# Heads of three feed-forward blocks run tile by tile in the tail of the attention ahead of them

## What is computed

```
x = x + xattn0(layernorm(x))   # 32 heads, q and k RMS-normalised, added mask, output matrix
x = x + ffn0(layernorm(x))     # softmax routing of 8; (x * in_scale) @ sign(W).T * out_scale + bias
x = x + xattn1(layernorm(x))   # one narrow head
x = x + ffn1(layernorm(x))     # base plus a Fourier-coded low-rank update
x = x + xattn2(layernorm(x))   # 32 heads, mask and position bias
x = x + ffn2(layernorm(x))     # base plus 8 gated rank-16 adapters (softmax minus a threshold)
x = x + xattn3(layernorm(x))   # 32 query heads on 4 key heads
x = x + ffn3(layernorm(x))     # base plus 8 rank-16 adapters, the best two by a router
```

## Time and profile before

| | |
|---|---|
| median of 3 runs | 2523.36 us (2516.17 to 2525.8) |
| the profiled execution | 2523.6 us, its span 2521.8 us |
| mean granted TensorE clock | 0.953 |
| busy share: PE, PEld, DVE, ACT, POOL | 91%, 51%, 52%, 46%, 20% |
| chain that ended last, by engine | PE 62%, DVE 13%, ACT 11%, issue 11%, POOL 2%, DMA 1% |

### The profile page before, as it was taken

How to read it: one execution, slowest core, us unless ns; L and a number is a source line. 1 busy time by engine, 2 the same in 40 slices (tenths; PEclk the granted TensorE clock), 3 DMA queues, 4 the chain that set the end, 5 groups by cost and what they waited for, 6 DMA issues and landing times.

```text
span 2521.8 us, 40314 instructions
## 1 busy us (share of the span) xinstructions
PE 2285.4 (91%) x14182; PEld 1284.5 (51%) x14182; DVE 1315.1 (52%) x2618; ACT 1148.8 (46%) x2990; POOL 516.2 (20%) x889
## 2 busy tenths in 40 slices
PE   4899999999786788999999999998869899999979
PEld 2556555556432333555555555554634455555545
DVE  5566666666521144656556555655342455555551
ACT  4666665665211123555445555433222565555530
POOL 2333233232200011221212222111200121212130
PEclk9999999999778998999999999999879999999988
DMA  3111011010002121111111111100210110010000
GB/s 113 43 43 43 23 43 43 24 39 1 22 0 100 49 78 38 62 47 61 46 61 47 63 61 45 45 12 11 78 67 1 36 49 35 34 36 33 1 30 34
DMA packets 27622, 106.94 MB, mean 42 GB/s; under 512 B 4353, under 2 KB 12929, under 8 KB 17426
## 3 DMA queue, kind: packets, MB, share of 16 engines
q1 hardware_dynamic: 26962, 104.10, 11.7%
q10 hardware_dynamic: 448, 0.03, 0.0%
HBM read 102.03 MB, written 2.10 MB: 41 GB/s over the span
## 4 chain that ended last, share of the span: by engine, by line
PE 62%; DVE 13%; ACT 11%; issue 11%; POOL 2%; DMA 1%; ACTq 0%; DVEq 0%; POOLq 0%; SPq 0%
PE bank L84 16%; PE bank L86 15%; PE bank L85 15%; PE bank L1263 2%; ACT m_E L423 2%; PE bank L1592 2%; DVE m_x L867 2%; PE bank L614 2%; DVE m_Sm L821 2%; PE bank L1172 1%; ACT m_E L419 1%; PE bank L1377 1%; ACT m_arena L401 1%; DVE m_A L861 1%; ACT m_arena L296 1%
## 5 line engine op out<-in xcount | busy, mean ns | idle before, releaser
L767 DVE TENSOR_TENSOR m_arena<-bank,m_arena 128x512 f16<-128x512 f32 x320 | 221.1, 691 | 513.5 <-ACT m_arena L401 513.1
L84 PE MATMUL bank<-m_input_parts,m_arena 128*128 128x512 f16 x1088 | 418.5, 385 | 6.6 <-DVE m_arena L767 2.3
L85 PE MATMUL bank<-m_input_parts,m_arena 128*128 128x512 f16 x1088 | 418.2, 384 | 0.0
L86 PE MATMUL bank<-m_input_parts,m_arena 128*128 128x512 f16 x1088 | 418.1, 384 | 0.0
L423 ACT ACTIVATE m_E<-m_Sm,m_nmax 128x64 f32<-128x64 f32 (+1 forms) x512 | 185.4, 363 | 395.8 <-DVE m_nmax L838 219.9
L879 POOL TENSOR_TENSOR m_E<-m_E,m_rinv 128x512 f32<-128x512 f32 (+1 forms) x192 | 177.6, 925 | 871.3 <-DVE m_rinv L852 871.3
L401 ACT ACTIVATE m_arena<-bank 128x512 f16<-128x512 f32 x320 | 189.7, 593 | 237.9 <-PE bank L86 237.4
L84 PE MATMUL bank<-m_wo_t,m_A 128*128 128x512 f16 x768 | 293.3, 382 | 3.1 <-DVE m_x L867 3.1
L85 PE MATMUL bank<-m_wo_t,m_A 128*128 128x512 f16 x768 | 292.5, 381 | 0.0
L86 PE MATMUL bank<-m_wo_t,m_A 128*128 128x512 f16 x768 | 292.4, 381 | 0.0
L419 ACT ACTIVATE m_E<-bank,m_nmax,m_qk 128x128 f32<-128x128 f32 x256 | 113.7, 454 | 178.1 <-DVE m_nmax L809 178.1
(11 more groups left out here) (267 smaller groups left out, 4454.1 us busy)
## 6 DMA issues: line engine op xcount, KB each, us to landing
m_raw<-a_q SPq DMA_DIRECT2D x24, 1024.0 KB, 4.8
m_raw<-a_o SPq DMA_DIRECT2D x24, 1024.0 KB, 4.9
m_raw<-a_k SPq DMA_DIRECT2D x9, 1024.0 KB, 4.9
m_raw<-a_v SPq DMA_DIRECT2D x9, 1024.0 KB, 5.4
m_bias_in<-bias SPq DMA_DIRECT2D x64, 128.0 KB, 2.0
m_arena<-f_w SPq DMA_DIRECT2D x4, 1024.0 KB, 5.1
m_arena<-ctx_t SPq DMA_DIRECT2D x2, 2048.0 KB, 7.6
m_x<-x SPq DMA_DIRECT2D x2, 1024.0 KB, 7.0
```

The lines of the kernel that those rows point to most:

```text
L84: pe.matmul(out, lhs[0], rhs[0], start=first, stop=False)
L85: pe.matmul(out, lhs[0], rhs[1], start=False, stop=False)
L86: return pe.matmul(out, lhs[1], rhs[0], start=False, stop=last)
L767: ins = dve.tensor_tensor(self.dest(name, part, 1), self.shaped(name, bank[m % 2][:, :]), self.dest(name, part, 0), ALU.subtract)
```

## The change

`BinaryFFN` and `AdapterFFN` now derive from a new `TailFFN`, whose work on each tile stands in the events of period 8 of the attention ahead. `f_stat` is a tile's statistics and power, `f_norm` its normalising, transposes and copy, `f_logit` its narrow product, its copy and the bias addition. The gate's and A's products become one of 137 or 136 columns. The weights are loaded in the tail. `BinaryFFN` keeps x transposed, applies the input scale in that layout (eight-row products with 128 columns) and so has no transposes in its body; its output scale and main product get two banks each. `AdapterFFN` puts the base product in five banks, two of them filled in slot 7 of the tail, three more before the gates are needed. In `scales` the weight scale comes second in the chain, with a semaphore `w_fac` for the rest. The order in the list (the lines are those of `events`):

```diff
+            if t == 8 and slot == 0:
+                out.append(("f_stat", 0))
             if ok(b):
                 out.append(("scores", b))
+            if t == 8 and slot == 7:
+                out.append(("f_main", 0))
+            if t == 8:
+                out.append(("f_norm", slot))
+            if t == 8 and slot == 7:
+                out += [("f_main", 1), ("f_logit", 7)]
             if made is not None:
                 out.append(("w_sum", made, misc))
...
             if ok(b - 2):
                 out.append(("mix", b - 2))
+            if t == 8 and 1 <= slot < 7:
+                out.append(("f_logit", slot - 1))
+            if t == 8 and slot in (5, 6):
+                out.append(("f_gate" if slot == 5 else "f_route", 0))
             if ok(b - 3):
                 out.append(("out", b - 3))
+            if t == 8 and slot < 7:
+                out.append(("f_stat", slot + 1))
+            if t == 8 and slot == 6:
+                out.append(("f_logit", 6))
```

The shares of the engines in a tile:

```diff
+    def load_tail(self, sp):
+        s, a = self.s, self.att
+        sp.wait_ge(*a.s["proj_lo"].by(16 * a.NT))
+        sp.wait_ge(*a.s["misc_read"].by(a.misc_total))
+        for dst, src in self.small_loads():
+            sp.dma_start(dst, src).then_inc(s["w_in"].sem, 16)
+        for dst, src in self.wide_loads():
+            sp.dma_start(dst, src).then_inc(s["w"].sem, 16)
...
+    def tail_pool(self, pool, step, t):
+        k, s = self.k, self.s
+        if step == "f_stat":
+            pool.wait_ge(*s["stat"].by(t + 1))
+            pool.tensor_tensor(k.rstd[:, t:t + 1], k.var[:, t:t + 1], k.c_mhalf, ALU.pow).then_inc(s["rstd"].sem, 1)
+        elif step == "f_logit":
...
+            pool.tensor_tensor(k.x[:, t, :], k.x[:, t, :], self.bias[:, :], ALU.add).then_inc(s["xb"].sem, 1)
...
+    def tail_act(self, act, step, t):
+        k, s, bank = self.k, self.s, self.k.bank
+        if step == "f_norm":
+            act.wait_ge(*s["xt"].by(t + 1))
+            act.activation(self.xtf[:, :, t * P:(t + 1) * P], bank[t % 2][:, :].rearrange("p (c n) -> p c n", c=KC),
+                           ACT.Copy).then_inc(s["xt_s"].sem, 1)
+        elif step == "f_logit":
+            act.wait_ge(*s["lg"].by(t + 1))
+            act.activation(self.lg[:, t, :], bank[7][:, 0:self.G], ACT.Copy).then_inc(s["lg_s"].sem, 1)
...
+    def tail_dve(self, dve, step, t):
+        k, s, ch = self.k, self.s, self.ch
+        if step == "f_stat":
+            dve.wait_ge(*self.att.s["xadd"].by(UNITS - TILES + 1 + t))
+            dve.bn_stats(k.bn[:, t, :], k.x[:, t, :]).then_inc(ch.sem, 1)
...
+        elif step == "f_norm":
+            dve.wait_ge(*s["rstd"].by(t + 1))
+            dve.wait_ge(*s["xt"].by(t - 1))
+            dve.tensor_scalar(self.xn[:, t % 2, :], k.x[:, t, :], k.mv[:, t, 0:1], k.rstd[:, t:t + 1],
+                              ALU.subtract, ALU.mult).then_inc(s["xn"].sem, 1)
...
+    def tail_pe(self, pe, step, t):
+        k, s, bank = self.k, self.s, self.k.bank
+        if step == "f_norm":
...
+            pe.wait_ge(*s["xn"].by(t + 1))
+            pe.wait_ge(*s["xt_s"].by(t - 1))
+            for c in range(KC):
+                ins = pe.transpose(bank[t % 2][:, c * P:(c + 1) * P], self.xn[:, t % 2, c * P:(c + 1) * P], k.ident[:, :])
+            ins.then_inc(s["xt"].sem, 1)
+        elif step == "f_logit":
...
+            pe.wait_ge(*s["xt_s"].by(t + 1))
+            pe.wait_ge(*s["lg_s"].by(t))
+            for c in range(KC):
+                ins = pe.matmul(bank[7][:, 0:self.G], self.xtf[:, c, t * P:(t + 1) * P], self.narrow[:, c, :],
+                                start=c == 0, stop=c == KC - 1)
+            ins.then_inc(s["lg"].sem, 1)
```

TensorE's share of `BinaryFFN`'s body (its signs stand behind `f_norm` 1 to 4 on VectorE, the routing of tiles 0 to 3 in slots 5 and 6), and the order of `AdapterFFN` on TensorE:

```diff
+        for i in range(TILES + 1):
+            if i == 3:
+                self.turn_route(pe, 1)
             if i < TILES:
...
+                for c in range(KC):
+                    ins = pe.matmul(bank[4 + i % 2][:, c * P:(c + 1) * P], self.ics[:, c * P:(c + 1) * P], self.rt[:, tok],
+                                    start=True, stop=True)
+                ins.then_inc(s["insc"].sem, 1)
+                pe.wait_ge(*s["out_s"].by(i - 1))
...
+                pe.matmul(self.out_bank(i), self.rt[:, tok], self.ocs, start=True, stop=True).then_inc(s["outsc"].sem, 1)
+            if i >= 1:
                 j = i - 1
                 pe.wait_ge(*s["y"].by(j + 1))
+                pe.wait_ge(*s["x"].by(j - 1))
...
+    def main_bank(self, t):
+        return self.k.bank[2 + t % 5][:, :]
...
+        for t in range(2, 5):
+            self.base(pe, t)
+        pe.wait_ge(*s["xt_s"].by(TILES))
+        turn(0)
+        turn(1)
         for t in range(TILES):
             pe.wait_ge(*s["ht_s"].by(t + 1))
+            pe.matmul(self.main_bank(t), self.ht[:, t % 2, :], self.bm[:, :], start=False, stop=True).then_inc(s["main"].sem, 1)
             if self.follower and t % 2 == 0 and t // 2 < self.follower.NP:
                 self.follower.sum_ahead(pe, t // 2)
+            if t + 2 < TILES:
+                turn(t + 2)
+            if t + 5 < TILES:
+                self.base(pe, t + 5)
```

The scale chain:

```diff
         tt(sc, tot, k.c_mhalf, ALU.pow, t)
+        tt(sc, sc, k.c_cw, ALU.mult, t, s["w_scale"])
         tt(inv, tot, k.c_half, ALU.pow, t)
-        tt(inv, inv, k.c_icw, ALU.mult, t)
-        last = lambda: tt(sc, sc, k.c_cw, ALU.mult, t, s["w_scale"])
...
     def low(self, dve, kind, j, par, count):
         dve.wait_ge(*self.s["w_hi"].by(count))
+        dve.wait_ge(*self.s["w_fac"].by(count))
```

More of the change, by code:

```diff
@@ L285, in emit @@
                          at(t, self.NK, self.NP + n - 1))
+                if isinstance(t, int) and t == 8 and slot == 1:
+                    self.next.load_tail(sp)
         self.periods(sp, emit)
@@ L519, in emit @@
             for e in events:
-                if e[0] == "w_sum":
+                if e[0][:2] == "f_":
+                    self.next.tail_pe(pe, e[0], e[1])
+                elif e[0] == "w_sum":
                     _, n, misc = e
@@ L744, in emit @@
             for e in events:
-                if e[0] == "w_sum":
+                if e[0][:2] == "f_":
+                    self.next.tail_dve(dve, e[0], e[1])
+                elif e[0] == "w_sum":
                     _, n, misc = e
@@ L912, in scales @@
             tt(k.tmp, k.tmp, k.joint[:, 1:2], ALU.mult, t)
[L913 to L921, removed]
+            tt(k.qk[:, kp], k.tmp, k.c_scale, ALU.mult, t, fac)
+        else:
+            tt(inv, inv, k.c_icw, ALU.mult, t, fac)
     def pool_ahead(self, pool):
@@ L961, in emit @@
             for e in events:
-                if e[0] == "w_sum":
+                if e[0][:2] == "f_":
+                    self.next.tail_pool(pool, e[0], e[1])
+                elif e[0] == "w_sum":
                     _, n, misc = e
@@ L1380, in pe, with __init__, small_loads, wide_loads @@
                 self.follower.sum_ahead(pe, t // 2)
[L1383 to L1403 removed]
+class AdapterFFN(TailFFN):
+    def __init__(self, k, layer, att, dram):
+        n = P + (9 if layer == 2 else 8)
+        regions = [[k.arena, 12288, 13312], [k.arena, 16384, 24576]] if layer == 2 else \
+            [[k.arena, 12288, 16384], [k.joint_parts[:, 2 * KC * TOK:].bitcast(FP32), 0, 4096]]
+        super().__init__(k, f"f{layer}", ["iota", "hw", "ht", "ht_s", "out"], att, dram, n, regions)
+        self.layer = layer
+        self.w = self.take([KC, D])
+        self.bm = self.take([D])
+        self.hw, self.ht = self.take([TILES, P]), self.take([2, P])
+        self.z9, self.e9, self.z, self.e, self.g2, self.m8, self.oh = (self.take([72]) for _ in range(7))
+        self.idx, self.idf = self.take([64]), self.take([64])
+        self.nm, self.sm, self.thr, self.p1, self.p2 = (self.take([8]) for _ in range(5))
+        self.bthr, self.iota = self.take([1]), self.take([8])
+    def small_loads(self):
+        d = self.dram
+        out = [(self.narrow[:, :, :], d["narrow"]), (self.bias[:, :], d["bias"].partition_broadcast(P)),
+               (self.bm[:, :], d["bm"])]
+        if self.layer == 2:
+            out.append((self.bthr[:, :], d["bthr"].partition_broadcast(P)))
+        return out
+    def wide_loads(self):
+        return [(self.w[:, :, :], self.dram["w"])]
@@ L1562, in dve, with base @@
                     self.follower.low_ahead(dve, t // 2)
+    def main_bank(self, t):
+        return self.k.bank[2 + t % 5][:, :]
+    def base(self, pe, t):
+        s, a = self.s, self.att.s
+        if t == 0:
+            pe.wait_ge(*s["w"].by(16))
+            pe.wait_ge(*a["exped"].by(UNITS))
+        if t == 2:
+            pe.wait_ge(*a["turned_lo"].by(UNITS))
+            pe.wait_ge(*a["mixed_lo"].by(UNITS))
+            pe.wait_ge(*a["xadd"].by(UNITS))
+        pe.wait_ge(*s["xt_s"].by(t + 1))
+        pe.wait_ge(*s["x"].by(t - 4))
+        for c in range(KC):
+            pe.matmul(self.main_bank(t), self.xtf[:, c, t * P:(t + 1) * P], self.w[:, c, :], start=c == 0, stop=False)
@@ L1586, in turn @@
```

(13 more changed lines are left out.)

374 lines of the change are left out of this document (194 added, 180 removed).

## The result

| | before | after |
|---|---|---|
| median | 2524.07 us (20 runs, 2515.43 to 2526.95) | 2529.72 us (20 runs, 2523.03 to 2533.69) |
| span of the profiled execution | 2521.8 us | 2530.6 us |
| mean granted TensorE clock | 0.953 | 0.947 |

The ratio is 1.0025, with a 95% interval of 1.0018 to 1.0032: slower by a quarter of a per cent. The forecast was 2516, slightly faster.

What follows compares the result with a forecast made beforehand. Serial heads at a low clock make the blocks long; interleaved tails become one VectorE-TensorE loop. Tails +88.4, clock +42, blocks -134.5, weight scale -3 sum to -7.1 us: forecast 2516 us, own range 2500 to 2540, wider range 2472 to 2555.

Steps and rivals of the forecast that it cites:

- `BinaryFFN`'s block: Feed-forward block behind the first tail: 51.4 us instead of 110.2, saving 58.8, with 3 for starting at the lower clock level.
- the adapter blocks: AdapterFFN blocks: middle one 45.0 us instead of 78.3, last one 39.7 instead of 82.1.
- What bounds, and the loop: Attention tails: side-by-side work of VectorE and TensorE becomes one loop, slots with scores 8.7, 10.9 and 8.7 us.
- Rival C: Tails: the loop doesn't close, slots grow by statistics and hand-overs only, 1.6 us each; 2420 us, chance 0.07.
- The last three slots: Slots 4 to 6 of a tail: no scores, but exposed power and normalising beside POOL's bias addition; 8.5 us each.
- The clock, 2.0 us a slot: Tails: TensorE's idling lowers its clock, costing 2.0 us in each of 21 slots, 42 us.
- Rival A: Tails: the clock level holds and tails grow by their work alone; 2474 us, chance 0.17.
- Rival B: Tails: the lower clock lasts through each burst, 4.9 us in place of 2.0 in 21 slots; 2577 us, chance 0.15.
- Hidden pieces: Tails: ScalarE's copies, POOL's power and bias addition, signs and loads mostly covered; loads cost 0, at worst 5 us once.
- The blocks: Three feed-forward blocks behind the tails: savings of 58.8, 33.3 and 42.4 us, 134.5 in sum.
- The five banks: AdapterFFN blocks: five banks pay by letting the base products run ahead of the gates.
- The scales, -3: Earlier weight scale: most of ScalarE's 28.0 us wait lies beside TensorE work; -3 us, ends -8 and 0.

Runs made afterwards that it cites:

- run 6: Kernel after with ten 128 x 512 float16 matmuls on TensorE ahead of each tile's transposes (tiles 0 to 6): 2496.3 us, ratio 0.9895.
- run 3: Kernel after with TensorE's transposes of a tile and ScalarE's copy of them moved to the end of the slot, behind out: 2425.6 us, ratio 0.9615.
- run 9: Kernel after with AdapterFFN's base product in two banks instead of five, only slot 7's bases ahead of the gates: 2548.2 us, ratio 1.009.
- runs 1 and 2: New scale chain alone on the kernel before: 2515.2 us, ratio 0.9969; kernel after with the old scale chain: 2542.9 us, ratio 1.008.
- runs 6 and 8: Kernel after with ten matmuls ahead of each tile's transposes: 128 x 512 float16, 2496.3 us; float32 of 128 x 128 by 8 columns, 2534.9 us.
- run 7: Kernel after with fifteen 128 x 128 float32 transposes of the identity ahead of each tile's transposes: 2499.5 us, ratio 0.9903.
- run 2: Kernel after with the old scale chain (weight scale last, no w_fac): 2542.9 us, ratio 1.008.

## Why the prediction was wrong

The mechanisms held, and what failed are sizes in the sum, most of them by a little and to the same side. `BinaryFFN`'s block was put at 51.4 us and took 58.8; the adapter blocks took 4.2 more than forecast; the clock was put at 2.0 us a slot and cost about 2.3; the last three slots of a tail were put at 8.5 us and take 9.0 at the upper clock; and the second tail's first slot was 3.1 us longer. Only the term outside tails and blocks erred the other way.

**What bounds, and the loop.** Right. The slot closes into one loop through both engines, as the timelines of the first section show, and its three lengths are within 0.25 us of the forecast (run 6). Rival C is refuted for this order of the queue, for the reason given against it; its 2420 is nearly what run 3 (2425.6) reached once that order was changed.

**The last three slots, forecast 8.5 each.** With the wide matmuls the nine of them take 88.3 us in place of 76.5. Four (12.16, 11.05, 9.98 and 9.97) still had a clock of 0.72 to 0.85; the five at 1.00 are 8.6 to 9.5, on average 9.0. So some 5 us of the 11.8 are the loop and the other 7 are clock. For the loop a row of the kernel after has the reason. VectorE's normalising takes 1.48 us while GpSimd adds the bias, 0.54 elsewhere, so 0.94 more, where I had taken 0.3 as half of a difference read in an eight-tile batch. GpSimd's timeline and VectorE's, in the fifth slot of the first tail:

```profile
674.85 1.26 POOL L1141 TENSOR_TENSOR m_x<-m_x,m_arena 128x512 f32<-128x512 f32 x1
```

```profile
674.91 1.48 DVE L1165 TENSOR_SCALAR m_arena<-m_x,m_mv,m_rstd 128x512 f32<-128x512 f32 x1 [0.67 <-POOL m_rstd L1136]
```

The second attention's first slot was 3.1 us longer as well (13.24 against 10.1), because tile 0's statistics come 3.1 us after its addition, behind the last work of period 7. Finally, the second tail of before was cut 3.1 us short. That overstated its growth and cancelled this.

**The clock, 2.0 us a slot.** A little low: 42 us forecast, 37 to 49 measured and 48 by the estimate of run 6, which is 2.3 a slot. It was no single value: the same slot of the third tail takes 8.57 or 10.24 us, and slots of the first take 10.0, 11.9 or 13.1 against 8.60. Rival A (the level holds) is refuted. Rival B (the whole burst at 1.2 GHz) is true of single slots, as the one shown, 4.5 us longer than at the upper level, near its 4.9. Its break-even was 2.3 us a slot, which is about what the clock cost. So B's sign came out, with single slots and not every slot at its price.

**Hidden pieces.** ScalarE's copies put no wait on TensorE in the slot shown, and the loads cost nothing that shows: in the second tail the slot with the loads, at 160 GB/s, takes 13.99 us and the next one, with none, 13.82. GpSimd's pieces did cost what the forecast had put on the path, and the bias addition beside the normalising more than that.

**The blocks: -134.5 forecast, -123.0 measured.** This is the largest miss, and 7.4 us of its 11.5 are `BinaryFFN`: 58.8 us in place of 51.4. TensorE's timeline in that block:

```profile
711.72 1.12 PE L1176 MATMUL bank<-m_ident,m_arena 128*128 128x128 f32 x4 [3.33 <-DVE m_arena L1165]
713.52 1.88 PE L1185 MATMUL bank<-m_arena,m_input_parts 128*128 128x8 f32 x8 [0.69 <-ACT m_input_parts L1147]
715.33 2.07 PE L1329 MATMUL bank<-m_arena 8*128 8x128 f32 x8
...
722.45 5.93 PE L1342 MATMUL bank<-m_arena 128*128 128x512 f32 x8
...
747.42 3.70 PE L1342 MATMUL bank<-m_arena 128*128 128x512 f32 x8
751.05 1.15 PE L1329 MATMUL bank<-m_arena 8*128 8x128 f32 x8
752.04 1.02 PE L1336 MATMUL bank<-m_arena 8*128 8x512 f32 x2
```

A tile takes 5.57 us (3.63 + 0.99 + 0.95, start to start), not 5.2; eight of them are 3 us. The other 4 are the start: everything down into the first main product ran at 1.2 GHz (the transposes 1.12 against 0.60, the eight narrow products 1.88 against 0.95 at 707.44, two tiles' scales 7.12 against 3.88, the main product 5.93 against 3.70). That is 6.9 us, where I had allowed 3. The adapter blocks were 2.9 and 1.3 us over their forecasts. The five banks paid 12.9 us in the last block and 4.6 in the middle one (run 9), where some 10 in each were expected.

**The scales, -3.** Too small: -7.7 alone, -13 as an undo (runs 1 and 2). I had called most of the wait hidden, and about half to three quarters of what was removed reached the time.

**The sum.** +10.2 in the tails, +11.5 in the blocks and -5.8 in the rest turned -7.1 into +8.8. Neither of the two large terms was off by as much as a tenth; but the result was the small difference of 130 and 137 us. An error of 6% in either decides the sign. The range (2472 to 2555) said that, and the measured +0.25% lies in what I called the same, but the chance of 0.42 for faster against 0.23 for slower leaned on a difference that the terms couldn't carry. That the time came out within 14 us of the forecast owes something to luck: the 21.7 us of error in tails and blocks were cut to 15.9 by the term that erred the other way.

## What to carry to other kernels

When work is interleaved into a running pipeline, place each engine's share of a step by itself: an in-order queue should meet a step when its input is ready, not when the producing engine starts it. Here one event moved behind `out` on TensorE and one behind the scores on GpSimd turned +0.25% into -4.2%. When a forecast is the difference of two terms of over 100 us each, the order of the queue is the thing to question before the sizes of the terms.

## What the runs showed of the hardware

- Ten eight-column float32 products per gap left the clock at 0.72 to 0.83 although TensorE was busy 85% of the time (204.4 of 241.4 us); ten 512-column products brought it to 0.93 to 0.95 (runs 6 and 8), and fifteen float32 transposes to 0.90 to 0.95 (run 7). The idle time left before the next transposes was much the same, 1.10, 1.17 and 1.65 us.
- The price of idling is not smooth: the second slot of the third tail takes 8.58 us in run 2 and 10.25 in the kernel after, with the same instructions and the same 2.64 us of idle time before the transposes.
- A normalising of 128 x 512 float32 on VectorE takes 0.54 us, or 1.48 beside GpSimd's addition of the same size.
